# Cross-attention and expert FFN: context's 32 x 32 blocks turned from the copy in SBUF and exchanged within SBUF

## What is computed

```python
# per batch, after layernorm of x over its last axis
q = softmax(heads(Wq @ x), over head dim) * scale        # 8 heads of 64
k, v = split(Wkv @ context)
k = softmax(heads(k), over the 1024 columns)
ctx = k @ v^T        # per head, 64 x 64
out = Wout @ (ctx^T @ q) + b_out
x = x + (out - mean) * rsqrt(var + 1e-5) * g             # over the 128 rows

# then, after layernorm over the last axis, for each of the 128 rows of a batch
scores = xf @ Wr.T; gates = softmax(top 16 of 64 scores)
out = sum over experts of gate * (xf @ A^T) @ B^T * 2
x = x + out
```

## Time and profile before

| | us |
|---|---|
| median of three runs | 1841.13 (1836.73 to 1843.48) |
| the profiled execution | 1843.23 |
| its span | 1841.5 |
| TensorE busy | 1775.7, 96% |
| VectorE busy | 1482.1, 80% |
| ACT busy | 1039.0, 56% |
| POOL busy | 1213.3, 66% |

### The profile page before, as it was taken

One profiled execution on the slowest core, in us unless ns is written; L12 is line 12 of the kernel. 1 busy time (PEld: TensorE's weight loads), 2 busy tenths in 40 slices (PEclk: granted clock), 3 DMA queues, 4 the chain that ended last, 5 costly groups with the idle time before them and its releaser, 6 DMA issues.

```text
span 1841.5 us, 29053 instructions
## 1 busy us (share of the span) xinstructions
PE 1775.7 (96%) x9564; PEld 1530.6 (83%) x9564; DVE 1482.1 (80%) x1983; ACT 1039.0 (56%) x1267; POOL 1213.3 (66%) x584
## 2 busy tenths in 40 slices
PE   4999999999999999999999879999999999999998
PEld 3788888888888888888888769988999999999987
DVE  5899999999999999999999967777777777777751
ACT  3888888888888888888888742222222222222210
POOL 3878787887878787878878726554555555555541
PEclk9999999999999999999999989999999999999999
DMA  6243333324242333333333454444444444444441
GB/s 155 61 98 84 82 87 90 90 76 103 73 106 72 88 91 81 87 90 90 77 92 109 140 172 138 161 160 154 163 155 164 158 159 161 158 159 160 152 136 59
DMA packets 295917, 215.94 MB, mean 117 GB/s; under 512 B 215168, under 2 KB 257792, under 8 KB 295872
## 3 DMA queue, kind: packets, MB, share of 16 engines
q1 hardware_dynamic: 282224, 191.76, 35.9%
q0 software_dynamic: 4608, 16.78, 3.2%
q10 hardware_dynamic: 9040, 6.82, 1.3%
HBM read 148.18 MB, written 71.30 MB: 119 GB/s over the span
## 4 chain that ended last, share of the span: by engine, by line
PE 76%; issue 9%; DVE 7%; POOL 4%; ACT 2%; DMA 2%; SPq 0%; DVEq 0%; POOLq 0%; ACTq 0%
PE ps L52 22%; PE ps L54 22%; PE ps L53 21%; PE ps L1300 6%; PE ps L1290 5%; DVE k_min L940 2%; DVE m_lo L970 1%; POOL rstd_c L548 1%; POOL hT_lo L563 1%; ACT m_hi L692 1%; POOL o_blk L554 1%; DMA g<-in_L_xattn_g 0%; DMA work<-x_turn 0%; DVE w_ra_lo L980 0%; ACT ek L668 0%
## 5 line engine op out<-in xcount | busy, mean ns | idle before, releaser
L533 POOL TENSOR_TENSOR eq<-eq,q_inv 128x1024 f32<-128x1024 f32 x128 | 242.5, 1901 | 154.4 <-DVE q_inv L936 154.4
L537 POOL TENSOR_TENSOR kT_lo<-kT,kT_hi 128x1024 fp32r<-128x1024 f32 x128 | 305.9, 2399 | 34.7 <-ACT kT_hi L650 31.3
L558 POOL TENSOR_TENSOR xT_lo<-work,xT_hi 128x1024 fp32r<-128x1024 f32 x32 | 76.4, 2387 | 313.2 <-ACT xT_hi L744 313.2
L52 PE MATMUL ps<-w_ra_hi,xT_hi 128*128 128x384 f32 (+1 forms) x768 | 251.9, 328 | 2.3 <-POOL xT_lo L558 2.2
L53 PE MATMUL ps<-w_ra_lo,xT_hi 128*128 128x384 f32 (+1 forms) x768 | 251.2, 327 | 0.0
L54 PE MATMUL ps<-w_ra_hi,xT_lo 128*128 128x384 f32 (+1 forms) x768 | 251.2, 327 | 0.0
L52 PE MATMUL ps<-w_b_hi,hT_hi 128*128 128x512 f32 x512 | 203.5, 397 | 3.6 <-POOL hT_lo L563 3.6
L54 PE MATMUL ps<-w_b_hi,hT_lo 128*128 128x512 f32 x512 | 201.3, 393 | 0.0
L53 PE MATMUL ps<-w_b_lo,hT_hi 128*128 128x512 f32 x512 | 200.9, 392 | 0.0
L657 ACT ACTIVATE qh<-ps,k_inv 128x1024 fp32r<-128x1024 f32 x128 | 142.9, 1116 | 71.7 <-PE ps L1290 65.7
L548 POOL TENSOR_TENSOR rstd_c<-var_c,minus_half 128x32 f32<-128x32 f32 x32 | 173.4, 5420 | 10.0 <-DVE var_c L1006 10.0
(11 more groups left out here) (141 smaller groups left out, 4707.2 us busy)
## 6 DMA issues: line engine op xcount, KB each, us to landing
x_sb<-in_x SPq DMA_DIRECT2D x64, 512.0 KB, 4.6
ctx_hi<-in_ctx POOLq DMA_DIRECT2D x32, 512.0 KB, 4.1
ctx_sb<-in_ctx SPq DMA_DIRECT2D x32, 512.0 KB, 3.9
ctx_blk<-in_ctx SPq DMA_DIRECT2D x512, 32.0 KB, 2.3
attention_out<-o_sb SPq DMA_DIRECT2D x32, 512.0 KB, 2.7
o_sb<-attention_out SPq DMA_DIRECT2D x32, 512.0 KB, 4.6
x_turn<-x_blk SPq DMA_DIRECT2D x32, 512.0 KB, 2.7
work<-x_turn SPq DMA_DIRECT2D x128, 128.0 KB, 2.8
```

Of the source, the lines that this page charges most:

```text
L52: pe.matmul(out, stat_hi, mov_hi, start=first, stop=False)
L533: pool.tensor_tensor(v, v, per_row(q_inv[:, i, :], 2 * HEADS, DH), ALU.mult).then_inc(q_normed, 1)
L537: pool.tensor_tensor(kT_lo[:, i % 2, :, :], kT[:, i % 2, :, :], kT_hi[:, i % 2, :, :].bitcast(F32), ALU.subtract).then_inc(kT_lo_ready, 1)
```

## The change

Context is loaded once less. VectorE now turns the blocks of ctx_sb, the copy that is there anyway, and writes them to ctx_blk grouped by q, the group of columns (`blocks_by_group`). Then SP issues 16 DMAs from SBUF to SBUF, each of which moves 32 partitions x 256 elements (1 KB runs) from group c of ctx_blk to group q of cT (`exchange_context`). ACT and POOL read cT through `turned_blocks` and write cT_hi and cT_lo through `turned`. The semaphore c_exchanged counts the 16 DMAs of a batch (256 a batch). ACT's cT_hi waits for it, and so do VectorE's turn of the next batch and block_rows(0); SP's next load of ctx_sb waits for the turn too.

```diff
--- before.py
+++ after.py
@@ -196,7 +196,7 @@
         z_folded, z_hi_ready, z_lo_ready = sem("z_folded"), sem("z_hi_ready"), sem("z_lo_ready")
 
         ctx_loaded = [sem(f"ctx_loaded{i}") for i in range(2)]
-        blk_loaded = [sem(f"blk_loaded{i}") for i in range(2)]
+        c_exchanged = sem("c_exchanged")
         x_loaded = [sem(f"x_loaded{i}") for i in range(2)]
         o_stored = [sem(f"o_stored{i}") for i in range(2)]
 
@@ -382,16 +382,17 @@
         def _(sp):
             def load_context(b, p):
                 wait_for(sp, ctx_lo_ready, b - 1)
+                wait_for(sp, c_turned, b - 1)
                 sp.dma_start(ctx_sb[p][:, :], context[b]).then_inc(ctx_loaded[p], 16)
 
-            def load_blocks(b, p):
-
-                wait_for(sp, c_turned, b)
+            def exchange_context(b):
+
+                wait_for(sp, cT_lo_ready, b)
+                sp.wait_ge(c_turned, b + 1)
                 for q in range(QB):
-                    dst = ctx_blk[BLK * q:BLK * q + BLK, :].rearrange("p (m c j) -> p m c j", m=NCH, j=BLK)
                     for c in range(QB):
-                        src = context[b][BLK * c:BLK * c + BLK, :].rearrange("i (m q j) -> i m q j", m=NCH, j=BLK)
-                        sp.dma_start(dst[:, :, c, :], src[:, :, q, :]).then_inc(blk_loaded[p], 16)
+                        sp.dma_start(cT[q * BLK:(q + 1) * BLK, c * 2 * P:(c + 1) * 2 * P],
+                                     ctx_blk[c * BLK:(c + 1) * BLK, q * 2 * P:(q + 1) * 2 * P]).then_inc(c_exchanged, 16)
 
             def load_x(b, p):
                 wait_for(sp, xn_ready, b - 1)
@@ -439,7 +440,9 @@
 
                 sp.wait_ge(o_stored[0], 16 * (LAST // 2))
                 sp.wait_ge(ctx_lo_ready, LAST)
+                sp.wait_ge(c_turned, LAST)
                 load_o(0, 0)
+                exchange_context(LAST)
                 sp.wait_ge(k_made, CH * LAST)
                 sp.wait_ge(q_made, 4 * LAST)
                 for n in range(4):
@@ -463,13 +466,13 @@
                     load_x(s + 2, par)
                 if edge and s == LAST:
                     first_rows()
+                if on("C", s, edge) and not (edge and s == LAST):
+                    exchange_context(s)
                 if on("K", s, edge):
                     place_b(s)
                 if on("O", s, edge):
                     sp.wait_ge(o_copied, s - 2 + 1)
                     sp.dma_start(o_dram[s - 2], o_sb[:, par, :]).then_inc(o_stored[par], 16)
-                if not edge or 0 <= s + 1 < BATCHES:
-                    load_blocks(s + 1, 1 - par)
                 if edge and s == BATCHES:
                     load_o(2, 0)
                     turn_rows(0)
@@ -517,8 +520,7 @@
 
             def context_turned_lo(b):
                 pool.wait_ge(cT_hi_ready, b + 1)
-                pool.tensor_tensor(cT_lo[:, :, :].rearrange("p a b -> p (a b)"), cT[:, :],
-                                   cT_hi[:, :, :].rearrange("p a b -> p (a b)").bitcast(F32),
+                pool.tensor_tensor(turned(cT_lo), turned_blocks(cT[:, :]), turned(cT_hi).bitcast(F32),
                                    ALU.subtract).then_inc(cT_lo_ready, 1)
 
             def x_lo(b, p):
@@ -712,9 +714,9 @@
                 act.copy(xn_hi[p][:, :], xn[:, :]).then_inc(xn_hi_ready, 1)
 
             def context_turned_hi(b):
-                act.wait_ge(c_turned, b + 1)
+                act.wait_ge(c_exchanged, 256 * b + 256)
                 wait_for(act, t_part, 4 * b)
-                act.copy(cT_hi[:, :, :].rearrange("p a b -> p (a b)"), cT[:, :]).then_inc(cT_hi_ready, 1)
+                act.copy(turned(cT_hi), turned_blocks(cT[:, :])).then_inc(cT_hi_ready, 1)
 
             def weight_hi(n):
                 act.wait_ge(w_turned, n + 1)
@@ -971,9 +973,9 @@
                                   ALU.subtract).then_inc(m_lo_ready, 1)
 
             def turn_context(b, p):
-                dve.wait_ge(blk_loaded[p], 16 * 8 * (b - p) + 256)
-                wait_for(dve, cT_lo_ready, b)
-                dve.transpose(cT[:, :], ctx_blk[:, :]).then_inc(c_turned, 1)
+                dve.wait_ge(ctx_loaded[p], 8 * (b - p) + 16)
+                wait_for(dve, c_exchanged, 256 * b)
+                dve.transpose(blocks_by_group(ctx_blk[:, :]), blocks_in_order(ctx_sb[p][:, :])).then_inc(c_turned, 1)
 
             def weight_lo(n):
                 dve.wait_ge(w_hi_ready, n + 1)
@@ -992,7 +994,7 @@
                 dve.wait_ge(o_loaded[p], 8 * (u - p) + 16)
                 wait_for(dve, y_ready, u)
                 if isinstance(u, int) and u == 0:
-                    dve.wait_ge(c_turned, BATCHES)
+                    dve.wait_ge(c_exchanged, 256 * BATCHES)
                 dve.transpose(o_blk[:, :], o2_sb[p][:, :]).then_inc(o_blocked, 1)
 
             def sum_squares(u):
```

## The result

The changed kernel takes 2035.57 us (median of four runs, 2034.24 to 2036.12) against 1841.74 before, measured beside it: a ratio of 1.1046, with a 95% interval of 1.1029 to 1.1063. The loss is 194 us. The forecast was 1884 us, in a range that ended at 1915.

What follows compares the result with a forecast made beforehand. The prediction took TensorE, busy 96% of the span, to bound the kernel. Its terms, 36 + 6.5 + 0.5 = 43 us on the profiled 1843.2, gave 1886.2, or 1884 us against the median; range 1846 to 1915.

Steps and rivals of the forecast that it cites:

- The bound: First stage's loop: TensorE, busy 197.69 of 200 us, bounds it; its idle time caps any gain at about 12 us.
- which chain the delay enters: Each batch: k_min, exponential of keys block 2, m_hi, m_lo, then TensorE's add_output; a delay there delays the batch.
- a longer wait for m_lo: Sign on TensorE in the loop: it would wait for m_lo some 1.2 us longer per batch.
- the block loads were hidden: SP, each batch: removing 16 block loads, issued in 11.92 us ahead of need, saves nothing on the path.
- the layouts cost nothing: Turn, cT_hi and cT_lo: the other layout adds nothing, as the mixing stage's 1235 against 1236 ns on VectorE showed.
- Rivals B and C: B: exchange fits before cT_hi's deadline, 1848 us, chance 0.20. C: block loads were in the way, 1836 us, chance 0.09.
- the price of an issue: SP's exchange in each batch: 0.38 us per issue, bounds 0.33 and 0.44, so the last of 16 goes out at 540.4.
- part 3: Exchange added on the path: cT_hi waits for 16 transfers, exponential 1.2 us later per batch, 36 us over 30 batches.
- rival D: Exchange copies are slow, by queueing or 0.75 us per issue: 2028 us, likelier 1910 to 1940; chance 0.13.
- The collision: Each batch: the exchange's end meets POOL's 512 KB ctx_hi load, issued at 539.29, so it lands at 543.4.
- Last batch: VectorE's block_rows(0) waits 7.0 us for the exchange; 6.5 us charged, bounds 4 and 8.
- First batch: Exchange lands by about 37.4, cT_hi done by 38.5 against the exponential's start at 38.30: 0.5 us at most.

Runs made afterwards that it cites:

- the run of cT_hi moved and last buffer: Changed kernel with cT_hi after the third query_hi in ACT's list and the last batch's turned blocks in xn_lo's buffer: 1843.47 us against 1842.56, ratio 1.0008.

## Why the prediction was wrong

**What held.** The bound, and which chain the delay enters: the exponential of keys block 2, then TensorE, with 1.09 us to swallow (the deadline of 7.56 us after the turn is confirmed by 8, 12, 14 and 16 transfers, which give 0, 1.8, 2.6 and 3.8 us of delay). It is the exponential itself that TensorE waits for, at queries block 3, whose PSUM pair it frees; the sign that the prediction named, a longer wait for m_lo, didn't show: that wait is gone (0.25 us before). That the block loads were hidden and their removal saves nothing: the run of cT_hi moved and last buffer, 1.0008. So the rule of the Trainium skill, page "DMA: Bandwidth & Descriptors", section "Specifications", that the prediction set against them (512 bytes as the least transfer for line rate) changes no time here: whatever their runs of 128 bytes cost the DMA engines, nobody waited for it. That the layouts cost nothing: the turn is at 1235 ns. Rivals B and C are out.

**The step that failed: the price of an issue** (part 3, "I take 0.38, between the two, since the new ones have 32 rows where those have 128"). It is 0.63 us: 10.07 for 16. My bounds of 0.33 and 0.44 came from rows of other forms; I reasoned that fewer rows make an issue cheaper, which the runs don't bear out, and I left the dearest row out of the bounds. The block loads have 16 issues of 32 rows too, and a row of before gives them as 11.92 us, 0.75 each. I used that only in rival D. With 0.63, and the measured landing of 1.8, the sum's own line gives 534.67 + 15 x 0.63 + 1.8 = 545.9, cT_hi done at 547.0 and the exponential 3.7 us late: 111 us in place of 36.

**The step that was missing: the clock.** I charged a gap on TensorE at its length. At 3.7 us it costs 5.9, since the clock that is granted afterwards is 0.50 for some 6 us; filling the gap took 58 us off. At 1.4 to 2.4 us it appears in only 3 of 58 batches. The kernel before has no such gap in its loop, and its clock there is 1.00. But its first batch showed the pattern. A window over it, from its turn of context to just past the next one, and the start of TensorE's timeline in it:

```profile
28.15:59.50 31.35, 22.27 (x97) 16.76 (x96) 24.28 (x29) 18.81 (x23) 19.86 (x10) 0.89 0.30 70
```

```profile
34.07 0.80 PE L52 MATMUL ps<-ctx_hi,wk_hi 128*128 128x512 f32 x1 [4.29 <-DVE eq L925]
34.67 0.63 PE L53 MATMUL ps<-ctx_lo,wk_hi 128*128 128x512 f32 x1
...
39.56 0.51 PE L52 MATMUL ps<-wq_hi,xn_hi 128*128 128x512 f32 x1 [2.56 <-ACT ek L668]
...
40.65 0.63 PE L53 MATMUL ps<-wq_lo,xn_hi 128*128 128x512 f32 x1
```

TensorE idles for 4.29 us ahead of a keys block, and the matmuls behind soon start 0.42 us apart. After the next gap, of 2.56 us, four matmuls start at full speed, and then the clock falls again. The mean clock of the batch is 0.89. I had read that batch for its waits alone, and had no term for the clock in the sum. The Trainium skill, page "TensorE: Matmul & The Clock Gate", section "Part 1: The HAM clock gate (the "warmup" mystery)", says that the clock is halved in idleness and that activity releases it. The trace agrees, with 0.50 behind the gap of 3.7 us.

**Rival D** named the mechanism (an issue as dear as the block loads') and 2028 us, near the 2035.57. The agreement is partly luck: it had 0.75 us per issue and a landing of 2.3, together 2.3 us a batch too much, and no clock, 2.1 us too little. Two errors made up for the third. I gave it 0.13, and called a third of its price likelier.

**The collision.** "The end of the exchange falls exactly there": it didn't, as the issues run past it. In a batch with 8 transfers and cT_hi held up for 0.84 us it can be seen, and it is inside the margin. With 16 the last transfer is issued 5 us after ctx_hi's load and lands in 1.8 us.

**The ends.** Last batch 6.5 us charged, 12.3 measured, by the same price of an issue: VectorE's wait is 10.6 us, not 7.0. First batch 0.5 charged, 4.3 measured.

**The sum put right:** 30 x 3.8 for the wait = 114, 30 x 2.1 for the clock = 63, 12 for the last batch, 4 for the first: 193 of 194 us. The term for the clock is read from the batch times (37.5 and 35.4 us); the whole run with the gap filled gained 58 us.

## What to carry to other kernels

A chain of small DMAs costs its issues in series, and where the rows at hand give different prices (here 0.33, 0.44 and 0.75 us) and none has the new form, the range has to reach to the dearest. Sixteen issues in series don't fit in 7.6 us, five through DRAM do. An instruction that gains a wait should go in its engine's list to where its input is there already and its output is still early: here one move gave back 181 of 194 us. And a gap on the engine that bounds the kernel isn't priced by its length alone; ask what its clock does behind it.

## What the runs showed of the hardware

- TensorE's granted clock behind the gap ahead of queries block 3, in the 30 batches of the loop of each run. Gaps of 3.6 to 4.5 us (16 transfers): 0.50 from the first matmul, in every batch, for some 6 us. Gaps of 2.3 to 2.4 us (14 transfers): 1.00 behind 27, 0.50 behind one; its two longer gaps, 3.25 and 3.38 us, were both followed by 0.50. Gaps of 1.4 to 1.9 us (12 transfers): 1.00 behind 28, 0.50 behind two. With the gap filled by matmuls: 1.00.
- The length of the gap alone doesn't decide: behind one of 1.81 us the clock is 0.50, behind one of 1.94 us it is 1.00. What else does isn't shown here.
- Issues from SP, back to back, in one batch of one trace: 0.615 us for 32x256 within SBUF (0.63 in the changed kernel), 0.49 from DRAM, 0.57 for 64x256, 0.62 for 16x512; in the same kernel 0.44 for 32x4x256 from DRAM.
- A copy of 32 KB within SBUF lands in 1.8 us (median), a block load of the same size from DRAM in 2.3 (median). The twelfth copy of a batch, issued 2.4 us after a load of 512 KB on GpSimd's queue, landed in 2.3.
